# A four-layer block on one core: softplus sums moved to accumulating transfers, a fifth state scaled by ScalarE, and two groups of VectorE rows moved around the scans

## The reference, cut to what matters

```
xv = silu(conv(xn @ W_in) + conv_b)             # 256 channels
ssm = xv @ W_x                                   # dt_raw (8), B (16), C (16)
delta = softplus(dt_raw @ W_dt + b_dt)
dA = exp(delta * A);  dBx = delta * B * xv       # 16 states per channel
h[t] = dA[t] * h[t-1] + dBx[t]                   # along the 512 tokens
y = sum over states of h * C + xv * D ;  s = y @ W_out
g = silu(FFN(xn)),  FFN = (silu(xn@wg) * (xn@wu)) @ wd       # 384 hidden
x = x + s * g
```

## Time and profile before

| | us |
|---|---|
| median of 3 runs | 787.35 (785.91 to 788.26) |
| the profiled execution | 789.01 |
| its span | 787.2 |
| VectorE busy in the span | 664.6 |
| GpSimd busy in the span | 504.5 |
| ScalarE busy in the span | 480.7 |
| matrix engine busy in the span | 667.2 |

### The profile page before, as it was taken

How to read it: one execution, slowest core, us unless ns; L and a number is a source line. 1 busy time by engine, 2 the same in 40 slices (tenths; PEclk the granted TensorE clock), 3 DMA queues, 4 the chain that set the end, 5 groups by cost and what they waited for, 6 DMA issues and landing times. The chain is left out here.

```text
span 787.2 us, 13531 instructions
## 1 busy us (share of the span) xinstructions
PE 667.2 (85%) x3984; PEld 495.5 (63%) x3984; DVE 664.6 (84%) x1182; ACT 480.7 (61%) x942; POOL 504.5 (64%) x292
## 2 busy tenths in 40 slices
PE   1889889999899928797998988888989979987882
PEld 0865556566565513466777777677767768777682
DVE  5968867777566638899999999899999999999992
ACT  1655656666344434978587585685695785874540
POOL 1002661000244552099999999989999999999952
PEclk9999999999999966989999999999999999998896
DMA  8800110003022244622032042042041230420000
GB/s 217 258 1 15 41 40 13 0 0 83 26 74 67 63 69 57 214 109 81 28 130 74 30 148 81 4 148 79 11 164 53 83 116 31 128 76 28 14 1 14
DMA packets 40199, 56.48 MB, mean 72 GB/s; under 512 B 5960, under 2 KB 30032, under 8 KB 40144
## 3 DMA queue, kind: packets, MB, share of 16 engines
q1 hardware_dynamic: 31888, 48.42, 19.1%
q0 software_dynamic: 6528, 6.84, 3.9%
q10 hardware_dynamic: 1728, 0.57, 0.4%
HBM read 46.08 MB, written 9.74 MB: 71 GB/s over the span
## 5 line engine op out<-in xcount | busy, mean ns | idle before, releaser
L1644 DVE TENSOR_TENSOR_SCAN xnT_all<-psum,nfT_all 128x1024 f32<-128x1024 f32 x128 | 285.3, 2270 | 2.7 <-issue 2.4
L1241 PEld LDWEIGHTS psum<-W_out,xnT_all 128*128 128x128 f32 x2048 | 243.8, 196 | 31.0 <-issue 29.0
L1241 PE MATMUL psum<-W_out,xnT_all 128*128 128x128 f32 x2048 | 246.0, 280 | 9.0 <-DVE acc L1660 9.0
L1394 ACT ACTIVATE psum<-delta,A 128x511 f32<-128x511 f32 x256 | 163.3, 678 | 39.2 <-DVE xnT_all L1644 38.4
L1226 POOL TENSOR_TENSOR nfT_all<-nf_rows,du 128x1024 f32<-128x1024 f32 x63 | 146.8, 2358 | 32.7 <-DVE nfT_all L1703 31.5
L1226 POOL TENSOR_TENSOR nfT_all<-attn_all,du 128x1024 f32<-128x1024 f32 x64 | 149.9, 2366 | 0.0
L569 POOL DMA_INDIRECT moe_dram<-xnT_all x40 | 38.3, 957 | 122.2 <-ACT xnT_all L825 122.2
L1660 DVE SCALAR_TENSOR_TENSOR acc<-psum,Cc,acc 128x128 f32<-128x128 f32 x352 | 96.7, 340 | 8.8 <-PE psum L1241 8.8
L558 POOL DMA_INDIRECT xs_dram<-nf_rows,pos x32 | 33.5, 1046 | 75.8 <-DVE pos L879 57.0
L1241 PE MATMUL psum<-vo_all,wgu 128*128 128x512 f32 (+1 forms) x96 | 47.6, 619 | 27.4 <-DVE hff L1714 27.4
L1241 PE MATMUL psum<-vo_all,W_taps 128*128 (+4 forms) x128 | 60.3, 619 | 1.4 <-ACT vo_all L1412 0.7
(11 more groups left out here) (209 smaller groups left out, 1139.2 us busy)
## 6 DMA issues: line engine op xcount, KB each, us to landing
nf_rows<-bt_dram SPq DMA_DIRECT2D x32, 512.0 KB, 5.2
attn_all<-bt_dram SPq DMA_DIRECT2D x32, 512.0 KB, 3.5
xs_dram<-attn_all SPq DMA_DIRECT2D x4, 645.0 KB, 8.6
xnT_all<-xs_dram SPq DMA_DIRECT2D x40, 64.5 KB
x_all<-in_x_dram SPq DMA_DIRECT2D x8, 256.0 KB, 7.0
res_all<-moe_dram POOLq DMA_DIRECT2D x8, 256.0 KB, 4.5
out_dram<-ow SPq DMA_DIRECT2D x8, 256.0 KB, 2.4
gud<-in_gate_dram SPq DMA_DIRECT2D x1, 1024.0 KB, 5.9
```

The lines of the kernel that those rows point to most:

```text
L1241: return nc.tensor.matmul(o, l, r, start=start, stop=stop)
L1394: ins = nc.scalar.activation(dA[:, i % RA, k, 1:L], delta[:, p, h, 1:L], ACT.Exp, scale=A[:, h, 2 * q + k:2 * q + k + 1])
L1644: nc.vector.tensor_tensor_scan(hring[:, i % R, :, :].rearrange("p n l -> p (n l)"), dA[:, i % RA, :, :].rearrange("p n l -> p (n l)"), dbx ...
```

## The change

Three edits. The softplus sums become transfers that add into their destination (`accum_op=ALU.add`), issued from GpSimd's queue with a semaphore of their own, s_sp; ScalarE writes ln(1+exp(-abs)) straight into delta. State 11 joins ON_ACT. `conv_gate(0)` moves ahead of the first scan of step 0 and `conv_gate(1)` between its two scans; `ffn_hidden` moves between the two scans of its step, and works in place in `hff`.

```diff
-        ON_ACT = (5, 7, 9, 15)
+        ON_ACT = (5, 7, 9, 11, 15)
...
                     def softplus_high():
-
                         w("lg", 1)
                         w("rl", KH)
-                        w("delta", 0)
                         alone(pool)
-                        nc.gpsimd.tensor_tensor(lg[:, :, :], lg[:, :, :], rl[:, :, :], ALU.add).then_inc(S["sp"], 1)
+                        pool.dma_start(delta[:, 1 - p, :, :], rl[:, :, :], accum_op=ALU.add).then_inc(s_sp, 16)
 
                     def softplus_low():
                         w("e1", 1)
-                        nc.gpsimd.tensor_tensor(e1[:, :, :], ab[:, :, :], e1[:, :, :], ALU.add)\
-                            .then_inc(S["corr"], 1)
+                        alone(pool)
+                        pool.dma_start(e1[:, :, :], ab[:, :, :], accum_op=ALU.add).then_inc(s_sp, 16)
 
                     def deltas():
-                        w("sp", 1)
-                        w("corr", 1)
-                        pool.wait_ge(S["dA"], at(b, "dA", 0))
-                        pool.wait_ge(S["du"], at(b, "du", 0))
-                        nc.gpsimd.tensor_tensor(delta[:, 1 - p, :, :], e1[:, :, :], lg[:, :, :], ALU.add)\
-                            .then_inc(S["delta"], 1)
+                        pool.wait_ge(s_sp, b * 48 + 32)
+                        alone(pool)
+                        pool.dma_start(delta[:, 1 - p, :, :], e1[:, :, :], accum_op=ALU.add).then_inc(s_sp, 16)
 
                     def drives():
-                        w("delta", 1)
+                        pool.wait_ge(s_sp, (b + 1) * 48)
+                        alone(pool)
...
-                            if q == 1 and end:
-                                sum_scaled(b - 1, 2)
+                            if q in (1, 2) and end:
+                                sum_scaled(b - 1, q + 1)
                             if q == 3 and end:
-                                sum_scaled(b - 1, 3)
+                                sum_scaled(b - 1, 4)
                                 output()
...
-                def decays(b, p, q):
+                def decays(b, p, q, first=False):
-                    if q == 0:
+                    if q == 0 and first:
                         act.wait_ge(S["delta"], at(b, "delta", 1))
+                    elif q == 0:
+                        act.wait_ge(s_sp, b * 48)
...
                         if q == 0 and end:
-                            scale_state(b - 1, 1 - p, 3)
-                        if scan and 3 <= q < 6:
+                            scale_state(b - 1, 1 - p, 4)
+                        if scan and 3 <= q < 7:
                             scale_state(b, p, q - 3)
...
-                        scans(q)
+                        if q == 0 and prep and end:
+                            conv_gate(0)
+                        scans(q, (0,))
+                        if q == 0 and prep and end:
+                            conv_gate(1)
                         if scan and 3 <= q < 6:
                             ffn_hidden(q - 3)
+                        scans(q, (1,))
                         if q == 0:
-                            if prep and end:
-                                conv_gate(0)
-                                conv_gate(1)
                             if end:
```

More of the change, by code:

```diff
@@ L487, in attention_moe_mamba_ffn @@
         s_o = sem("p6_out_stored")
+        s_sp = sem("p6_softplus_summed")
         names6 = {"xv_ps": KH, "yh": KH, "tc": KH, "xv": KH, "ff_ps": KF, "tf": KF, "fa": KF, "hf": KF,
@@ L1045, in attention_moe_mamba_ffn @@
             tf = sb6("tf", [P, L])
-            fa = sb6("fa", [P, L])
             hff = sb6("hff", [P, KF, L])
@@ L1214, in round_ @@
                                 softplus_low()
+                            if q == 7 and prep:
+                                deltas()
                             if q == 7:
-                                if prep:
-                                    deltas()
                                 sum_scaled(b, 1)
@@ L1459, in C_out, with taken @@
                             .then_inc(S["C"], 1)
+                    def taken():
+                        if end:
+                            act.wait_ge(s_sp, b * 48)
+                        elif scan:
+                            act.wait_ge(S["delta"], at(0, "delta", 1))
                     def abs_relu(h):
                         w("dt_ps", h + 1)
-                        w("corr", 0)
                         w("lg", 0)
-                        w("delta", 0)
+                        taken()
                         nc.scalar.activation(ab[:, h, :], bank[bD[h]], ACT.Abs, bias=b_dt[:, h:h + 1])
@@ L1476, in ln_one_plus @@
                         w("ey", 1)
-                        w("delta", 0)
-                        nc.scalar.activation(lg[:, :, :], ab[:, :, :], ACT.Ln, bias=1.0).then_inc(S["lg"], 1)
+                        taken()
+                        nc.scalar.activation(delta[:, 1 - p, :, :] if scan else lg[:, :, :], ab[:, :, :], ACT.Ln, bias=1.0).then_inc(S["lg"], 1)
                     def one_plus():
                         w("ey", 1)
-                        w("delta", 0)
+                        taken()
                         nc.scalar.activation(e1[:, :, :], ab[:, :, :], ACT.Identity, bias=1.0).then_inc(S["t"], 1)
@@ L1515, in first_preparation @@
                         act.wait_ge(F["col"], 1)
-                        decays(b + 1, 1 - p, 0)
+                        decays(b + 1, 1 - p, 0, True)
                         turned(3)
@@ L1634, in ws, with scans @@
                         dve.wait_ge(S[n], at(b, n, c))
-                    def scans(q):
+                    def scans(q, halves):
                         if not scan:
                             return
-                        for h in range(KH):
+                        for h in halves:
                             i = 2 * q + h
@@ L1709, in ffn_hidden @@
                         ws("hf", k)
-                        nc.vector.scalar_tensor_tensor(fa[:, :], tf[:, :], 1.0, bank[bM[0]], ALU.add, ALU.mult)\
+                        ws("dn_ps", 0)
+                        nc.vector.scalar_tensor_tensor(hff[:, k, :], tf[:, :], 1.0, bank[bM[0]], ALU.add, ALU.mult)\
                             .then_inc(S["fa"], 1)
                         ws("fa", k + 1)
-                        ws("dn_ps", 0)
-                        nc.vector.scalar_tensor_tensor(hff[:, k, :], fa[:, :], 0.5, bank[bM[1]], ALU.mult, ALU.mult)\
+                        nc.vector.scalar_tensor_tensor(hff[:, k, :], hff[:, k, :], 0.5, bank[bM[1]], ALU.mult, ALU.mult)\
                             .then_inc(S["hf"], 1)
```

## The result

The changed kernel takes 779.91 us (median of 5 runs, 778.58 to 780.96) against 787.35 (785.91 to 788.26): a ratio of 0.991, 95% interval 0.989 to 0.993, so 7.4 us faster. Forecast were 775.3, in a range of 768 to 786. The time is that of the second rival (780.7), and so is the mechanism. The profiled execution took 780.36, its span 778.5 against 787.2.

What follows compares the result with a forecast made beforehand. VectorE's own list was taken to set the pace, with GpSimd at the same pace; both would reach about 53.1 us. Six rounds give 9.7, the first and last 2.4: 787.35 - 12.1 = 775.3, range 768 to 786.

Steps and rivals of the forecast that it cites:

- the second rival: GpSimd becomes the bound: at a landing of 7.4 us its round is 54.45, the time 780.7; chance 0.20.
- GpSimd runs at the same pace, and a gain on VectorE must be matched there: GpSimd's round before was 54.60 us against VectorE's 54.72, so a gain on one must be matched on the other.
- The pace is VectorE's own list, with 1.39 us of matrix engine in it: VectorE's 54.72 us round before: 53.33 of work back to back, 1.39 of waits for projections.
- VectorE's round 53.0, with a wait of 0.3 at the second gate and 0.4 at the second sum: VectorE's new round: a list of 52.29 us plus 0.7 of waits for the matrix engine's long run; bounds 52.3 to 53.7.
- Issue at 1.26 each: GpSimd's cost of issuing each of three accumulating transfers a round: 1.26 us, 3.8 in all (2.9 to 5.7).
- Landing 6.3: Time for a softplus transfer to land: 6.3 us, 4.5 plus 1.7 for a load of B; bounds 4.3 to 9.4.
- GpSimd's loss 0.4, its round 53.05: GpSimd's wait for landings beyond covers of 5.90 and 7.13 us: 0.4, added to a round of 52.65.
- The lead needed is 4.8, at scan 6: GpSimd must begin its round 4.8 us ahead of VectorE for dbx 6 to reach scan 6; it has 5.75.
- `deltas` starts 42.4 into GpSimd's round: Start of the `deltas` transfer, some 42.4 us into GpSimd's round, leaving ScalarE's first decays five microseconds of cover.
- Round 0 and the last give 1.2 each: The first and last rounds gain only state 11 and most of its gap: 1.2 us each, 2.4 together.
- The slower case: Landings at `deltas` and `drives` cost GpSimd more than the additions; break-even at 7.9 us, 797 at 8.7; chance 0.13.
- The Trainium skill's estimate of 3.2 us: Landing of a 512 KB transfer by the skill's formula: 3.2 us, so no wait and a GpSimd round of 52.65.

Runs made afterwards that it cites:

- no_transfers: The changed kernel with the three softplus sums back as GpSimd additions in place of transfers; ratio 1.000 to the kernel before.
- loads_held: The changed kernel with SP holding a round's last four loads of B until the three softplus transfers have landed; 770.87 us, ratio 0.979 to the kernel before.
- state_only: The kernel before with state 11 moved to ScalarE and GpSimd (and `ffn_hidden` in place); ratio 1.001 to the kernel before.
- order_only: The kernel before with only the gates and FFN rows moved (`ffn_hidden` in place); ratio 0.9935 to the kernel before.
- sum_first: The changed kernel with GpSimd's sum_scaled(b, 1) ahead of the third transfer instead of behind it; 771.17 us, ratio 0.980 to the kernel before.

## Why the prediction was right or wrong, point by point

- *GpSimd runs at the same pace, and a gain on VectorE must be matched there*: right. `no_transfers` gains nothing, and `loads_held` gives both.
- *"The pace is VectorE's own list, with 1.39 us of matrix engine in it"*: wrong. It is a ring of 54.7 through VectorE and the matrix engine, and state 11 alone, which the sum prices at 1.04 with its gap of 0.27, is worth nothing (`state_only`).
- *VectorE's round 53.0, with a wait of 0.3 at the second gate and 0.4 at the second sum*: right in time, 53.1 to 53.2; measured 0.61 and 0.36. I added two waits on the way round a ring; the ring itself gives the number, 53.0, and `order_only` reaches 53.1 to 53.2 with state 11 still on VectorE. So the number holds, but the part of it that state 11 was to bring is not there: its 1.04 came back as these waits.
- *Issue at 1.26 each*: too dear. By the starts it is 0.58 (575.44 to 576.02, 580.67 to 581.25). The nearest rows were runs of transfers one behind another, indirect ones; here a dbx follows, which starts while the issue still runs. The row at 4.95 for two shows that overlap, since the next start comes 4.65 later all the same.
- *Landing 6.3*: the step that failed. Alone it is 4.5 to 4.9, which the row of 256 KB had nearly right (4.5): twice the bytes in pieces eight times as long cost nothing. With a load of B beside it 7.2, and the second, with the load and the first transfer near, 8.4. I had counted the load at 1.7; it costs 2.7, and I had left out the transfer before, which may be the rest.
- *GpSimd's loss 0.4, its round 53.05*: measured 0 and 2.3 ahead of the third transfer in the first two rounds, then 3.0 to 3.8, and nothing at `drives` but once (0.50). The round is 54.5. The row's 3.36 leaves out the tail of the dbx pair ahead of it: by the starts the third issue comes 9.22 after the second (landing of this one 8.7), where issue and two dbx need 0.58 + 4.65, so the loss is 3.99. With it the prediction's own sum closes: 48.87 + 3 x 0.58 + 3.99 = 54.6. The second rival had 54.45 for a landing of 7.4: that it came so near is luck in part, since a dear issue and a short landing cancel in it.
- *The lead needed is 4.8, at scan 6*: right. It is there, and almost there alone, that scans wait.
- *`deltas` starts 42.4 into GpSimd's round*: its own terms, 14 dbx at 2.32, three sums at 1.23, 4.3 and two issues at 1.26, add up to 43.0. With five microseconds of cover that changes nothing, and no scan of the changed kernel waits for the decays.
- *Round 0 and the last give 1.2 each*: 1.0 and 1.3.
- *The slower case*: its price was right in kind, but break-even lay farther off than L = 7.9: a median of 8.4 still wins, since issues were cheaper and the third landing (5.5) was covered.
- *The Trainium skill's estimate of 3.2 us* ("DMA: Bandwidth & Descriptors", section "Anatomy of one DMA — SWDGE (gpsimd) path"): too low for this transfer; 4.5 is the least of any here, so about 1.3 more than the fit for a plain one. *The Trainium skill's rule on VectorE blocking descriptor writes* ("SBUF — State Buffer", section "SBUF: two separate sides"): no run here shows it; in `loads_held` no issue took over 1.23 beside a VectorE at full load.

The likeliest forecast missed by 4.6 us. The term that carried it off is the wait for the second landing, from round 2 on about 4.0 a round by the starts where I had 0.4; the issues, 1.7 where I had 3.8, gave 2 of that back.

## What to carry to other kernels

When an addition becomes a transfer, its price is not its issue but the landing under the traffic that runs beside it: see which loads are released by the same instruction that stands ahead of the issue, and hold back those that aren't due. When two engines run at one pace, ask which lead the faster may spend and how many rounds it lasts; a gain that dies out in the later rounds is a spent lead. And before taking work from the busy engine, find the ring of waits that sets the round, and whether the work lies in it; work outside the ring only buys waiting.

## What the runs showed that was not expected

A cover of 1.23 us moved by one place was worth 1% of the time (`sum_first`), as much as removing the collision (`loads_held`). Both kernels begin round 0 alike, with GpSimd waiting for ScalarE. With the cover GpSimd stays early and its second transfer stays clear of the first and of the load; without it, it slips within two rounds into a course that is 1.4 us a round slower. That the lateness feeds itself is how the rows read; no run shows it by itself.

The other surprise is that both the old order and the new one (the new one once the landing is out of the way) are paced by a ring through VectorE and the matrix engine (54.7 and 53.0), and that the one edit which took rows from VectorE, state 11, opened neither.
